# An attention kernel whose per-head stacks and diagonals are filled by transfers through memory instead of by TensorE, for three of its four quartets of batches

## The chip, the cores and the metric

The kernel runs on one core of one Trainium2 chip. The metric is the device time of one execution in microseconds (us); lower is better. Engines: PE (TensorE), DVE (VectorE), ACT (ScalarE), POOL (GpSimd), SP (SyncE, which here only issues transfers). Line numbers (L714) are those of the kernel before.

## What is computed

```python
# x, ctx: (16, 128, 128) f32; 16 heads of 8; mask_BxS2 all ones
x = x + cross_attention(layernorm(x), ctx, ctx, mask, Wq, Wk, Wv, Wo)
#   Q = split_heads(q @ Wq.T), K, V likewise from ctx
#   scores = where(mask == 0, -1e9, Q @ K.T / sqrt(8)); softmax; @ V; @ Wo.T
x = x + moe_ffn(layernorm(x), wg, w1, w3, w2)
#   8 experts, top 2 of softmax(x @ wg.T), silu(x @ w1.T) * (x @ w3.T) @ w2.T
```

## The kernel before

The 16 batches are taken as NQ = 4 quartets of QB = 4 batches; a quartet is T = 512 tokens. Attention runs in rounds u = 0 to 4. In round u PE computes two things side by side, in steps (b, g) with b = 0 to 4 and g = 0 to 3 (a "tick" is 4b + g): for b below 4 the second scores ("S2", L697 and L700) of batch b of quartet u-1, from which ACT takes the exponential (L940); for b of 1 and more the first scores ("S1", L714) of batch b-1 of quartet u, from which DVE takes the maxima (L1431). S1 is used only for the maxima of the softmax; S2 computes the scores again, in the other orientation, with the maxima subtracted by a matmul against m_bd. The maxima of a quartet are turned by PE at the start of the next round (`transpose_maxima`, L545), copied by DVE (mT, L1374) and spread by POOL into m_bd in four steps (L1048). `values` (L673) multiplies the probabilities with V, and three more small steps (L556, L562, L569) finish a batch.

Heads have 8 dimensions, and 4 heads share a matmul. A score must be as exact as fp32, but the matmuls take fp32r, which keeps fewer bits; so each operand is split into a high and a low part. A **stack** `st[:, k, g, :]` (k = 0 queries, 1 keys; g = 0 to 3) holds for each of 4 heads 32 rows: the 8 dimensions three times (high, high and low, or high, low and high) and rows for the mask's bias. A **diagonal** `bd_slot(k, n)` holds for batch n the same rows in block diagonal form, 128 x 2048, so that one matmul of 512 columns gives four heads' scores at once. Its zero blocks are cleared once (`clear_diagonal`, ACT L825), and transfers fill the blocks.

How stacks and diagonals come about before: at the start of each round u below 4, `front(u)` (L624) computes all 8 stacks of quartet u on PE: 4 key stacks of 4 matmuls (one for the bias) and 4 query stacks of 3, each 128x512 (`split_product`, L539), with weights whose columns are repeated threefold (`ws_hi`, `ws_lo`). For each stack ACT copies the high part (`st_hi`, L812 and L913) and DVE combines high and low (L1393). SP then issues, per batch and side, 4 transfers of 64 KB each from stack to diagonal (`block_diagonal`, L424 to L436); 3 diagonals for each side rotate. `st` is double: quartet u is written to `st[:, u % 2]`. The tokens of quartet u+1 are normalised by DVE at b = 3 of round u, turned by PE at (4, 0) (`transpose_tokens`), split at (4, 1) and (4, 2) (x_hi on ACT, x_lo on DVE L1361); the masked context is split on ACT at (4, 3) and on DVE after the round (`context_rest`, L1184).

What sets the order: each engine runs its list in order, semaphores join them. SP's list is that of the round loop from L438; PE's is `front(u)` and the double loop over b and g. The banks of PSUM for the small products alternate by a table (`slot_order`). After round 4 comes the expert part (from about 183 us on), which the change leaves alone save for where some tiles lie.

Of the kernel before, what the change touches and what calls it, by code (L numbers as in the profile page):

```python
# [42 lines left out]
P = 128  # L43
# [44 lines left out]
C_N = C_TILE + NT  # L88
# [3 lines left out]
def constants():  # L92
# [28 lines left out]
    hi, lo = split_constant(NEG)  # L121
    for j in range(NJ):
        c[0, C_BIAS + R * j + 24] = hi
        c[0, C_BIAS + R * j + 25] = lo
# [18 lines left out]
def slot_order():  # L143

    order = [("V", 0), ("xT", 0)]
    for u in range(NQ):
        if u:
            order += [("V", u), ("MT", u - 1)]
        order += [("st", u, k) for k in range(2 * NG)]
        order += [("xT", u + 1)] if u + 1 < NQ else [name for tick in EARLY_FILLS for name in EARLY_FILLS[tick]]  # L150
# [21 lines left out]
STACKS = [(0, 0), (1, 0), (1, 1), (1, 2), (1, 3), (0, 1), (0, 2), (0, 3)]  # L172
# [3 lines left out]
def stacks(u):  # L176

    return sorted(STACKS, reverse=True, key=lambda s: s[0]) if u == 0 else STACKS

def program(nc, x, ctx_in, mask, Wq, Wk, Wv, Wo, wg, w1, w3, w2, consts, xg, ys, out):
    slot, bank_of, turn, uses = slot_order()
    with ExitStack() as stack:
# [16 lines left out]
        nokeep = sb("nokeep", [P, 2, T], F32R)  # L201
# [37 lines left out]
        st = sb("st", [P, 2, 2, NG, T], F32R)  # L239
        bd = sb("bd", [P, 6, NG * NJ * P], F32R)  # L240
# [22 lines left out]

        def bd_slot(k, n):

            return bd[:, 3 * (1 - k) + n % 3, :].rearrange("p (g j q) -> p g j q", g=NG, j=NJ)
# [3 lines left out]
        w3_lo = st[:, 0, 1, :, :].rearrange("p g (m c) -> p (g m) c", c=P)  # L270
        wt_hi = [wt[:, 0], wt[:, 2], wt[:, 4]]
        wt_lo = [wt[:, 1], w3_lo, wt[:, 5]]
# [19 lines left out]
        flat = st[:, :, :, :, :].rearrange("p a b g t -> p (a b g) t")  # L292
        g_hi = [flat[:, 8 + k, 0:I] for k in range(GR)]
        g_lo = [flat[:, 11 + k, 0:I] for k in range(GR)]
        t_hi = [flat[:, 14, k * CT:(k + 1) * CT] for k in range(2)]
        t_lo = [flat[:, 15, k * CT:(k + 1) * CT] for k in range(2)]
# [57 lines left out]
        kbd_ready = [sem(f"kbd_ready{k}") for k in range(3)]  # L354
        qbd_ready = [sem(f"qbd_ready{k}") for k in range(3)]
# [25 lines left out]
        def stacks_in(engine, u, is_k):  # L381

            for k, (kind, _) in enumerate(stacks(u)):
                if kind == is_k:
                    taken(engine, ("st", u, k))

        def diagonal_in(engine, k, n):

            engine.wait_ge((kbd_ready if k else qbd_ready)[n % 3], 16 * NJ * (n // 3 + 1) - (32 if k and n % 3 == 0 else 0))
            if k and n == 0:  # L390
                engine.wait_ge(first_half, 32)
# [17 lines left out]
        def _(sp):  # L409
# [11 lines left out]
            for k, w in enumerate((w1, w3)):  # L421
                sp.dma_start(raw[k], w).then_inc(in_w13, 16)

            def block_diagonal(k, n):  # L424

                u, b = divmod(n, QB)
                stacks_in(sp, u, k)
                if n >= 3:

                    sp.wait_ge(s1_full if k else s2_full, NG * (n - 2))  # L430
                else:
                    sp.wait_ge(bd_cleared, 3 if k else 6)
                for j in range(2 if k and n == 0 else NJ):
                    rows = slice(R * j, R * (j + 1))
                    sp.dma_start(bd_slot(k, n)[rows, :, j, :].bitcast(F32), st[rows, u % 2, k, :, b * S:(b + 1) * S].bitcast(F32)  # L435
                                 ).then_inc((kbd_ready if k else qbd_ready)[n % 3], 16)  # L436

            for u in range(NQ + 1):  # L438
                if u == NQ:
                    sp.wait_ge(work_full, slot["V", NQ - 1] + 1)  # L440
                    sp.wait_ge(ck_ready, NQ)
                    sp.dma_start(raw[2], w2).then_inc(in_w2, 16)

                for k, b in ((1, 0), (1, 1), (1, 2), (0, 3), (1, 3)):
                    if k and u < NQ:
                        block_diagonal(1, QB * u + b)
                    if not k and u >= 1:
                        block_diagonal(0, QB * (u - 1) + b)
                if u < NQ:
                    block_diagonal(0, QB * u)  # L450
                    block_diagonal(0, QB * u + 1)
                    block_diagonal(0, QB * u + 2)
# [64 lines left out]
        def _(pe):  # L517
# [106 lines left out]
            def front(u):  # L624
# [14 lines left out]
                if u >= 1:  # L639
                    transpose_maxima(u - 1)  # L640
                for k, (is_k, g) in enumerate(stacks(u)):
                    if k in (1, 3) and u >= 2:
                        (heads_by_dim if k == 1 else project_out)(QB * (u - 1) - 1)
                    o = claim(("st", u, k))
                    if k < 2 and u:
                        pe.wait_ge(max_done, NG * QB * u)
                    if k == 0 and u == 0:
                        pe.wait_ge(ws_ready, 2)
                    if not is_k and g == 0:
                        taken(pe, ("xT", u))  # L650
                    if is_k and g == 0:
                        pe.wait_ge(cklo_ready, u + 1)
                        pe.wait_ge(mask_ready, u + 1)
                        if u == 0:
# [924 lines left out]
```

## Time and profile before

| | us |
|---|---|
| median of 2 runs | 274.03 (273.87 to 274.19) |
| the profiled execution's own time | 272.4 |
| its span, first to last instruction | 270.6 |
| mean granted clock of PE | 0.908 |

| engine | busy us | share |
|---|---|---|
| PE | 207.4 | 77% |
| DVE | 212.7 | 79% |
| ACT | 132.0 | 49% |
| POOL | 110.0 | 41% |

The shares are means over stages with different limits, so the stages have to be read one by one. The first S1 matmul of rounds 1, 2 and 3 starts at 49.78, 80.40 and 112.02 us of the span; round 4 starts near 141 us and ends near 181 us.

### The profile page before, as it was taken

How to read it: one execution, taken by the hardware profiler on the slowest of the kernel's cores; microseconds unless marked ns; L12 is line 12 of the kernel's file. 1: busy time of each engine (PE TensorE's matmuls, PEld its weight loads, DVE VectorE, ACT ScalarE, POOL GpSimd, SP SyncE). 2: the span in 40 equal slices, each digit the busy share in tenths (PEclk: the TensorE clock that was granted, in tenths of full speed). 3: DMA queues.
4: the chain of work that ended last, by engine and by line, in shares of the span. 5: the costliest groups of instructions: out<-in, count | busy, mean ns of one | idle time of the engine just before them, and what ended most of it. 6: DMA issues, size and time to landing. Idle time of an engine off the chain costs nothing.

```text
span 270.6 us, 5291 instructions
## 1 busy us (share of the span) xinstructions
PE 207.4 (77%) x1445; PEld 154.7 (57%) x1445; DVE 212.7 (79%) x619; ACT 132.0 (49%) x292; POOL 110.0 (41%) x122
## 2 busy tenths in 40 slices
PE   0795779899989989878749884427759999999810
PEld 0572267566756657555525553326658889888600
DVE  4869977498668896789787768786898778888796
ACT  5779037555475636635216773402435555655400
POOL 4401424040602107010749764627336556655630
PEclk9996589999999999999977999555999999999985
DMA  7974420344123320333260210035143322320807
GB/s 229 286 296 115 123 74 13 97 103 114 32 58 98 87 70 0 80 97 99 72 204 13 78 47 24 29 78 138 50 89 85 91 68 79 88 69 19 258 17 225
DMA packets 38108, 26.33 MB, mean 97 GB/s; under 512 B 4748, under 2 KB 35726, under 8 KB 37696
## 3 DMA queue, kind: packets, MB, share of 16 engines
q1 hardware_dynamic: 34848, 19.76, 26.9%
q0 software_dynamic: 2656, 5.40, 6.4%
q10 hardware_dynamic: 576, 0.83, 1.0%
q8 instruction: 13, 0.21, 0.3%
q14 instruction: 15, 0.12, 0.2%
HBM read 12.32 MB, written 6.31 MB: 69 GB/s over the span
## 4 chain that ended last, share of the span: by engine, by line
PE 53%; DVE 32%; issue 6%; DMA 4%; SPq 2%; ACT 2%; POOL 1%; DVEq 0%; ACTq 0%
PE bank L539 8%; DVE m_neg L1431 6%; PE bank L778 4%; PE bank L673 4%; PE bank L697 4%; PE bank L751 4%; PE bank L754 3%; PE bank L700 3%; PE bank L752 3%; PE bank L714 3%; PE bank L779 3%; PE bank L764 3%; DMA bd<-st 2%; DVE st L1393 2%; SPq L435 2%
## 5 line engine op out<-in xcount | busy, mean ns | idle before, releaser
L1431 DVE TENSOR_REDUCE m_neg<-bank 128x4 f32<-128x512 f32 x64 | 43.3, 683 | 14.4 <-PE bank L714 14.2
L1073 POOL DMA_INDIRECT ys<-big x39 | 38.2, 979 | 31.9 <-DVE big L1471 18.0
L940 ACT ACTIVATE big<-bank 128x512 f32<-128x512 f32 x64 | 36.9, 597 | 19.0 <-PE bank L700 18.7
L812 ACT ACTIVATE st<-bank 128x128 fp32r<-128x128 f32 (+1 forms) x78 | 21.9, 329 | 24.8 <-PE bank L764 15.4
L714 PE MATMUL bank<-bd,st 128*128 128x512 f32 x64 | 30.3, 497 | 4.6 <-DMA bd<-st 3.6
L1026 POOL DMA_INDIRECT xg<-rows,rows_i x24 | 24.3, 1011 | 22.8 <-DVE rows_i L1258 15.9
L697 PE MATMUL bank<-m_bd,ones_b 128*128 128x512 f32 x64 | 29.9, 468 | 2.9 <-ACT big L940 2.9
L1393 DVE SCALAR_TENSOR_TENSOR st<-st_hi,cst,bank 128x512 fp32r<-128x512 f32 x32 | 23.3, 748 | 9.6 <-ACT st_hi L812 7.3
L1048 POOL TENSOR_TENSOR m_bd<-mT,cst 128x512 fp32r<-128x512 f32 x16 | 17.3, 1108 | 33.0 <-DVE mT L1374 33.0
L700 PE MATMUL bank<-bd,st 128*128 128x512 f32 x64 | 25.8, 403 | 0.0
L982 ACT ACTIVATE big<-bank 128x256 f32<-128x256 f32 x39 | 15.0, 385 | 19.4 <-PE bank L754 19.4
L778 PE MATMUL bank<-bd,st 128*128 x78 | 22.5, 310 | 1.9 <-DVE big L1471 1.9
L1535 DVE TENSOR_TENSOR big<-big,bank 128x256 f32<-128x256 f32 x39 | 16.4, 421 | 9.4 <-ACT big L982 9.4
L751 PE MATMUL bank<-bd,st 128*128 x39 | 19.7, 505 | 4.8 <-DVE st L1459 4.8
L714 PEld LDWEIGHTS bank<-bd,st 128*128 128x128 f32 x64 | 13.8, 220 | 13.2 <-issue 6.8
L1009 POOL TENSOR_SCALAR ve<-mv 128x4 f32<-128x4 f32 (+2 forms) x9 | 2.4, 269 | 45.5 <-DVE mv L1100 40.9
L779 PE MATMUL bank<-bd,st 128*128 x78 | 20.3, 282 | 0.0
L697 PEld LDWEIGHTS bank<-m_bd,ones_b 128*128 128x128 f32 x64 | 12.8, 200 | 10.4 <-issue 5.7
L1464 DVE TENSOR_TENSOR st<-bank,st 128x256 fp32r<-128x256 f32 x39 | 16.5, 424 | 2.2 <-ACT st L812 1.3
L673 PE MATMUL bank<-big 128*32 128x128 f32 x512 | 17.3, 276 | 0.5 <-DVE x_all L1189 0.5
L778 PEld LDWEIGHTS bank<-bd,st 128*128 128x128 f32 x78 | 14.6, 188 | 4.7 <-issue 3.9
L1471 DVE TENSOR_REDUCE big<-bank 128x128 f32<-128x256 f32 x39 | 16.3, 418 | 0.4 <-PE bank L779 0.4
(175 smaller groups left out, 504.5 us busy)
## 6 DMA issues: line engine op xcount, KB each, us to landing
bd<-st SPq DMA_DIRECT2D x126, 64.0 KB, 2.0
big<-xg SPq DMA_DIRECT2D x39, 64.5 KB, 2.0
raw<-in_L_ffn_w SPq DMA_DIRECT2D x2, 1024.0 KB, 9.4
raw<-ys SPq DMA_DIRECT2D x6, 256.0 KB, 4.6
x_all<-in_x SPq DMA_DIRECT2D x4, 256.0 KB, 4.2
rows<-in_mask_BxS_if POOLq DMA_DIRECT2D x4, 256.0 KB, 5.0
ctx_all<-in_L_ffn_w SPq DMA_DIRECT2D x1, 1024.0 KB, 5.4
ctx_all<-in_ctx SPq DMA_DIRECT2D x3, 256.0 KB, 5.0
```

What stands on the lines that cost most here:

```text
L673: last = nc.tensor.matmul(ob[n % 2][R * j:R * (j + 1), half * P:(half + 1) * P], va[(n // QB) % 2][:, ((n % QB) * 4 + half * 2 + i) * NJ + ...
L697: nc.tensor.matmul(s2[k % 2][:, :], ones_b[:, b, :], m_bd[:, NJ * g:NJ * (g + 1), :].rearrange("p h q -> p (h q)"), start=True, stop=False)
L700: nc.tensor.matmul(s2[k % 2][:, :], st[:, (u - 1) % 2, 1, g, b * S:(b + 1) * S], bd_slot(0, n)[:, g, :, :].rearrange("p j q -> p (j q)"), ...
L714: nc.tensor.matmul(s1[k % s1_ring(u)][:, :], st[:, u % 2, 0, g, (b - 1) * S:b * S], bd_slot(1, n)[:, g, :, :].rearrange("p j q -> p (j q)" ...
L751: nc.tensor.matmul(both, t_lo[n % 2], first_high[:, :, bass.ds(col[n], I)], start=True, stop=False)
L778: nc.tensor.matmul(o, g_hi[n % GR][:, c * P:(c + 1) * P], w, start=(c == 0), stop=False)
L779: last = nc.tensor.matmul(o, g_lo[n % GR][:, c * P:(c + 1) * P], w, start=False, stop=(c == 1))
L940: nc.scalar.activation(prob[n % 2][:, NJ * g:NJ * (g + 1), :].rearrange("p h q -> p (h q)"), s2[k % 2][:, :], ACT.Exp, scale=SCALE).then_i ...
L1026: pool.indirect_dma_start(xg, bass.IndirectOffsetOnAxis(rows_i[:, n, k:k + 1], 0), sent_rows(n // QB)[:, n % QB, k, :], None, bounds_check ...
L1073: pool.indirect_dma_start(ys, bass.IndirectOffsetOnAxis(xt[n % XR][:, D:RW].bitcast(I32), 0), y_sb[n % YR], None, bounds_check=PAIRS - 1, ...
L1393: nc.vector.scalar_tensor_tensor(st[:, u % 2, is_k, g, :], st_hi[:, n % SH, :].bitcast(F32), cst[:, (C_CK if is_k else C_CQ):(C_CK if is_k ...
L1431: nc.vector.tensor_reduce(m_neg[:, H * (b - 1) + NJ * g:H * (b - 1) + NJ * (g + 1)], s1[k % s1_ring(u)][:, :].rearrange("p (j q) -> p j q" ...
```

## The change

Round 0 is as before. For quartets 1 to 3 (the diff's quartets 2 to 4) the 8 stacks are no longer computed:

- PE computes queries and keys once (`queries(u+1)` at tick (2, 2) of round u, `keys(u+1)` at (2, 3); 3 matmuls of 128x512 each), with compact weights `once_w` (two ACT copies after round 0's stacks).
- ACT copies the high parts (`queries_high`, `keys_high`, at (2, 3) and (3, 0)), DVE makes the low parts and the bias rows (`queries_rest`, `keys_rest`, ticks 12 and 13), into `staged`, which lies where the weights w1 and w3 are loaded.
- ACT issues four transfers of 512 KB to a new tensor `qk` in memory: `write_high` twice at (3, 1), `write_low` twice at (3, 3). `qk[u-1, k]` is [128, 4, 512]: each head dimension with its four rows.
- SP issues 4 transfers of 256 KB from `qk` for a whole stack side (`load_stack`) and 4 of 128 KB for the diagonals of a pair of batches (`diagonals`). `st` is single now, so `load_stack(u+1, 0)` waits until all S1 of quartet u are done, and `load_stack(u, 1)` until all S2 of quartet u-1 are. 8 diagonal buffers (2 pairs per side) take the place of 6.
- SP's order in a round: query diagonals of the pair 2u, key stack of quartet u, key diagonals of the first pair of quartet u+1, query stack of quartet u+1, query diagonals of pair 2u+1, key diagonals of the second pair. The loads of w1 and w3 move from the start to the end of this list in round 2.
- The preparation of the next quartet moves ahead: mean and variance to ticks 0 to 2 (for quartet 1 to before round 0's loop), masks to ticks 3 and 4, normalising to 5 and 6, `transpose_tokens` to (1, 3), the context's split to (1, 3) and tick 8, the tokens' to (2, 0) and tick 9.
- `clear_values(1)` moves to DVE's start; POOL clears the two new buffers (`memset` of 128x4096); some tiles of the expert part lie elsewhere.

```diff
+            def queries(u):
+                o = claim(("qc", u))
+                taken(pe, ("xT", u))
+                pe.wait_ge(once_ready, 1)
...
+            def write_high(u, k):
+                act.wait_ge(hi_staged, 2 * u - 1 + k)
+                places = qk[u - 1, k][:, 0:3:2, :] if k else qk[u - 1, k][:, 0:2, :]
+                act.dma_start(places, compact[k][0].unsqueeze(1).to_broadcast([P, 2, T])).then_inc(kc_written if k else qc_written, 16)
+
+            def write_low(u, k):
+                taken(act, ("kc" if k else "qc", u))
+                places = qk[u - 1, k][:, 1:4:2, :] if k else qk[u - 1, k][:, 2:4, :]
+                act.dma_start(places, staged[:, 3 * (1 - k) + 1:3 * (1 - k) + 3, :]).then_inc(kc_written if k else qc_written, 16)
...
+            def diagonals(k, m):
+                u, half = divmod(m, 2)
+                if m >= 2:
+                    sp.wait_ge(s1_full if k else s2_full, 2 * NG * (m - 1))
...
+                if u:
+                    sp.wait_ge(kc_written if k else qc_written, 32 * u)
+                else:
+                    stacks_in(sp, k)
+                tokens = slice(2 * S * half, 2 * S * (half + 1))
+                for j in range(NJ):
+                    rows = slice(R * j, R * (j + 1))
+                    source = rows_of(u, k, j)[:, :, tokens] if u else st[rows, k, :, tokens].bitcast(F32)
+                    sp.dma_start(bd_pair(k, m)[rows, :, j, :].bitcast(F32), source).then_inc((kbd_ready if k else qbd_ready)[m % 2], 16)
...
+            def load_stack(u, k):
+                sp.wait_ge(kc_written if k else qc_written, 32 * u)
+                sp.wait_ge(s2_full if k else s1_full, NG * QB * u)
...
+                for j in range(NJ):
+                    sp.dma_start(st[R * j:R * (j + 1), k, :, :].bitcast(F32), rows_of(u, k, j)).then_inc(kst_ready if k else qst_ready, 16)
...
+            for u in range(NQ):
+                if u:
+                    diagonals(0, 2 * u)
+                    load_stack(u, 1)
+                if u + 1 < NQ:
+                    diagonals(1, 2 * u + 2)
+                    load_stack(u + 1, 0)
+                if u:
+                    diagonals(0, 2 * u + 1)
+                if u + 1 < NQ:
+                    diagonals(1, 2 * u + 3)
+                if u + 2 == NQ:
+                    for k, w in enumerate((w1, w3)):
+                        sp.dma_start(raw[k], w).then_inc(in_w13, 16)
```

PE's wait before the first S1 of a round is now for `stack_loaded(pe, u, 0)` (4 landings of the query stack) and `diagonal_in` (4 landings of the pair of key diagonals).

## Rows read from the trace of the kernel before

**Rows 1.** Part 2 of the page, span in 40 slices.
```profile
PEclk9996589999999999999977999555999999999985
```

**Rows 2.** Stretches: length, busy PE, PEld, DVE, ACT, POOL; PEclk, DMA share, GB/s.
```profile
49.80:67.20 17.40, 17.04 (x185) 11.49 (x185) 14.54 (x38) 9.60 (x21) 3.13 (x4) 1.00 0.43 106
67.20:80.40 13.20, 11.74 (x54) 8.27 (x53) 8.79 (x19) 8.45 (x17) 4.40 (x4) 1.00 0.17 44
80.40:97.50 17.10, 16.62 (x185) 11.54 (x185) 14.21 (x37) 9.29 (x20) 2.57 (x3) 1.00 0.36 94
97.50:112.00 14.50, 12.08 (x55) 8.30 (x54) 11.35 (x32) 8.64 (x18) 5.66 (x6) 1.00 0.13 35
```

**Rows 3.** Chain that ended last, 62 to 83 us: start, length, what.
```profile
70.12 2.08 PE bank L539 x8
...
75.21 0.76 DVE st L1393
...
76.10 0.58 SPq L435
...
78.02 2.05 DMA bd<-st
...
80.40 0.47 PE bank L714
80.87 0.23 PE bank L697
```

**Rows 4.** Timeline, 62 to 98 us, by engine.
```profile
66.76 0.48 PE L714 MATMUL bank<-bd,st 128*128 128x512 f32 x1
...
69.36 4.40 POOL L1048 TENSOR_TENSOR m_bd<-mT,cst 128x512 fp32r<-128x512 f32 x4 [10.39 <-DVE mT L1374]
...
88.76 0.40 PE L697 MATMUL bank<-m_bd,ones_b 128*128 128x512 f32 x1
...
93.04 0.39 PE L700 MATMUL bank<-bd,st 128*128 128x512 f32 x1
...
96.15 0.68 DVE L1361 TENSOR_TENSOR x_lo<-bank,x_hi 128x512 fp32r<-128x512 f32 x1
...
97.39 0.48 PE L714 MATMUL bank<-bd,st 128*128 128x512 f32 x1
```

**Rows 5.** One line's instructions, L435 (issue of the diagonals).
```profile
L435 SPq DMA_DIRECT2D bd<-st x126: 585/601/1547, 19.3 to 149.2; - x126
...
DMA to landing us min/median/max: 2.0/2.0/4.5
```

**Rows 6.** Issues of part 6: KB each, median us from issue to landing.
```profile
out<-ctx_all SPq DMA_DIRECT2D x3, 256.0 KB, 3.1
```

**Rows 7.** Busy time by stretch where DMA share is near 1 (columns as Rows 2).
```profile
15.00:18.00 3.00, 3.00 (x13) 2.43 (x12) 1.82 (x3) 1.49 (x3) 0.00 (x0) 1.00 1.01 411
264.00:268.00 4.00, 0.00 (x0) 0.00 (x0) 3.72 (x14) 0.00 (x0) 0.00 (x0) 0.50 0.99 284
```

**Rows 8.** Busy time by single microseconds round clock changes (columns as Rows 2).
```profile
21.00:22.00 1.00, 0.00 (x0) 0.00 (x0) 0.96 (x2) 1.00 (x2) 0.10 (x1) 1.00 0.68 177
...
23.00:24.00 1.00, 1.00 (x3) 0.81 (x4) 1.00 (x1) 1.00 (x1) 0.00 (x0) 0.50 0.40 100
...
36.00:37.00 1.00, 1.00 (x9) 1.00 (x7) 1.00 (x2) 0.00 (x0) 0.00 (x0) 0.75 0.30 78
```

**Rows 9.** Chain that ended last, 138 to 150 us.
```profile
144.79 0.44 PE bank L700
...
145.75 0.62 ACT bd L812
```

**Rows 10.** Timeline, 0 to 50 us: round 0 and first product of round 1.
```profile
22.33 1.76 DVE L1158 MEMSET big<- 128x2048 f32 x1 [0.38 <-issue]
...
22.86 2.04 PE L714 MATMUL bank<-bd,st 128*128 128x512 f32 x4 [2.48 <-DMA bd<-st]
...
49.78 0.47 PE L714 MATMUL bank<-bd,st 128*128 128x512 f32 x1 [0.39 <-DMA bd<-st]
```

More of the change, by code:

```diff
@@ L121, in constants @@
     hi, lo = split_constant(NEG)
+    c[:, C_KB] = np.where(p % HD == 0, hi, np.where(p % HD == 1, lo, 0.0))
+    c[:, C_QB] = p % HD < 2
     for j in range(NJ):
@@ L379, in taken, with stacks_in, stack_loaded @@
             engine.wait_ge(into_sbuf(name), turn[name] + 1)
-        def stacks_in(engine, u, is_k):
-            for k, (kind, _) in enumerate(stacks(u)):
+        def stacks_in(engine, is_k):
+            for k, (kind, _) in enumerate(STACKS):
                 if kind == is_k:
-                    taken(engine, ("st", u, k))
-        def diagonal_in(engine, k, n):
-            engine.wait_ge((kbd_ready if k else qbd_ready)[n % 3], 16 * NJ * (n // 3 + 1) - (32 if k and n % 3 == 0 else 0))
-            if k and n == 0:
-                engine.wait_ge(first_half, 32)
+                    taken(engine, ("st", k))
+        def stack_loaded(engine, u, is_k):
+            if u:
+                engine.wait_ge(kst_ready if is_k else qst_ready, 16 * NJ * u)
+            else:
+                stacks_in(engine, is_k)
+        def diagonal_in(engine, k, n):
+            m = n // 2
+            if k and m == 0:
+                engine.wait_ge(first_ready[n], 16 * NJ if n else 32)
+                if n == 0:
+                    engine.wait_ge(first_half, 32)
+            else:
+                engine.wait_ge((kbd_ready if k else qbd_ready)[m % 2], 16 * NJ * (m // 2 + (0 if k and m % 2 == 0 else 1)))
         x_d = x.rearrange("(u b) s d -> u s b d", b=QB)
@@ L438, in _, with first_diagonal @@
[L438 to L452, printed above, removed]
+            def first_diagonal(n):
+                stacks_in(sp, 1)
+                sp.wait_ge(bd_cleared, 2)
+                for j in range(NJ if n else 2):
+                    rows = slice(R * j, R * (j + 1))
+                    sp.dma_start(bd_slot(1, n)[rows, :, j, :].bitcast(F32), st[rows, 1, :, n * S:(n + 1) * S].bitcast(F32)
+                                 ).then_inc(first_ready[n], 16)
@@ new lines, in rows_of @@
+            def rows_of(u, k, j):
+                return qk[u - 1, k].rearrange("(g j d) t c -> j (d t) g c", g=NG, j=NJ)[j]
+            def load_stack(u, k):
+                sp.wait_ge(kc_written if k else qc_written, 32 * u)
+                sp.wait_ge(s2_full if k else s1_full, NG * QB * u)
+                if u == 1 and not k:
+                    for m in range(2):
+                        diagonal_in(sp, 0, 2 * m)
+                for j in range(NJ):
+                    sp.dma_start(st[R * j:R * (j + 1), k, :, :].bitcast(F32), rows_of(u, k, j)).then_inc(kst_ready if k else qst_ready, 16)
@@ L638, in front @@
                     context_values(u)
[L639 removed]
                     transpose_maxima(u - 1)
[L641 to L647, printed above, removed]
+                    if u >= 2:
+                        heads_by_dim(QB * (u - 1) - 1)
+                        project_out(QB * (u - 1) - 1)
+                    return
+                for k, (is_k, g) in enumerate(STACKS):
+                    o = claim(("st", k))
+                    if k == 0:
                         pe.wait_ge(ws_ready, 2)
                     if not is_k and g == 0:
[L650 removed]
+                        taken(pe, ("xT", 0))
                     if is_k and g == 0:
[L652 to L655 removed]
+                        pe.wait_ge(cklo_ready, 1)
+                        pe.wait_ge(mask_ready, 1)
+                        pe.wait_ge(setup_ready, 2)
                     parts = (ws_hi[:, is_k, g, :], ws_lo[:, is_k, g, :])
                     if is_k:
[L658 removed]
+                        last = split_product(o[:, :], parts, (ck_hi[:, :], ck_lo[:, :]), (bias_w[:, :], nokeep[:, :]))
                     else:
@@ L722, in _ @@
                             (heads_by_query, heads_by_dim, project_out)[g - late](QB * (u - 1) + b - 2)
-                        if (b, g) == (4, 0) and u + 1 < NQ:
+                        if u + 1 < NQ and (b, g) == (1, 3):
                             transpose_tokens(u + 1)
+                        if u + 1 < NQ and (b, g) == (2, 2):
+                            queries(u + 1)
+                        if u + 1 < NQ and (b, g) == (2, 3):
+                            keys(u + 1)
                         if u + 1 == NQ:
@@ L1163, in _ @@
             clear_values(0)
+            clear_values(1)
             dve.wait_ge(in_x[0], 16)
```

283 lines of the change are left out of this document (175 added, 108 removed).

## The prediction, made before the changed kernel ran

> **What bounds the kernel now.** I read the page's 40 slices first, then the busy time by stretch, then the chain of waits round one turn of a round, then the timeline. The mean shares hide that rounds and the gaps between them have different limits. From the first S1 matmul of a round to its last, PE is the bound: busy 17.04 of 17.40 us and 16.62 of 17.10 us, DVE 14.5 and 14.2, ACT under 10 [rows 2]. In the gap that follows (13.2 us in the second, 14.5 us in the third) the transfer engines are almost empty, at shares of 0.17 and 0.13 [rows 2]. Its chain is: stack matmuls of 0.23 us each (28 of them, 6.4 us), the last stack on DVE 0.76, issues on SP of 0.58 and more, 2.05 us for the landing, then S1 [rows 3]. The first S1 matmuls stand at 49.78 [rows 10] and 80.40 us [rows 3], and the third stretch ends where the next one comes, at 112.0 [rows 2]: turns of 30.6 and 31.6 us. The change empties this gap of its matmuls. PE's clock is at the full 2.4 GHz from slice 7 to slice 21 [rows 1].
>
> I measure a turn from S3, the start of b = 3: in round 2 that is 88.76 us, 8.4 us after the first S1; the last S2 matmul ends at 93.4 (S3 + 4.7), and the last S1 begins at 97.39 (S3 + 8.6) [rows 4].
>
> **What is removed.** Per gap 28 matmuls (6.4 us of PE), 8 ACT copies, 8 DVE combines. What is then late on the compute side is POOL's m_bd, 4.40 us for its four parts, ending at 73.76 where the last S1 began at 66.76 [rows 4]: last S1 + 7.0, and S1 could start at + 7.6 (two S2 matmuls and a handover more). That would be S3 + 16.2, against 88.76 to 112.0 = S3 + 23.2 now. So the change can gain up to 7 us a turn there, if the data have landed by then.
>
> **What is added on the transfers' path.** ACT can issue the high parts only at (3, 1), after the exponential of (3, 0) and two copies: S3 + 1.9. An issue of this kind costs 0.60 us [rows 5]. The low parts wait in ACT's list for (3, 3): ACT takes them at S3 + 5.2 (4.4 by the exponentials' pace, 0.8 for what was put ahead of them) and is done at S3 + 6.4. Behind these issues stand the exponentials, on which PE's S2 depends, but at b = 3 the path runs through the transfers anyway. Bytes: 4 x 512 KB written, beside them the key stack of 1 MB (free to go after the last S2); after the writes have landed, 0.5 MB of key diagonals and 1 MB of query stack. Together 4.5 MB where the gap moved 13.2 us x 44 GB/s = 0.6 MB before [rows 2].
>
> No row has 2 KB pieces in both directions at full load. The nearest: 284 GB/s at share 0.99 with results read and written in 512 B pieces, and 411 GB/s at share 1.01 for weights in 8 KB pieces [rows 7]. I take 350, between them, and keep both ends. A 64 KB transfer lands 2.0 us after its issue [rows 5], a 256 KB one 3.1 [rows 6]; I put 1.2 us before the data and 0.6 after. Then:
> - writes and key stack: data from S3 + 3.1; 3.15 MB at 350 GB/s is 9.0 us, 0.3 us are lost before the low parts arrive: S3 + 12.4, landed S3 + 13.0;
> - SP issues 4 diagonals and 4 stack parts, 8 x 0.6 with 0.04 between; the last issue begins 4.5 us after, and lands 3.1 later: S3 + 20.6.
>
> At 411 GB/s it is S3 + 19.7; at 284 GB/s, S3 + 22.4. Even the fast end is later than POOL's S3 + 16.2: the bound of the gap changes from PE to the transfers.
>
 No row here shows a large one of that kind; by the page's figures the four parts of a stack would take 4.8 us, and the sum would be about 1.5 us longer a turn.
>
> **What is added in the round.** Six matmuls at 0.23 us [rows 3]: 1.4 us of PE, in a stretch that PE bounds; turning the tokens (0.45) moves from b = 4 to b = 1, into the part before S3: together 1.9 us, bounded by 0.5 (hidden in small waits) and 3 (DVE, whose 14.2 us get the low parts and bias rows, some 0.68 each [rows 4], and the context's 0.68: 16.7, so it is near the bound too).
>
> **The clock.** After 2.5 us without a matmul (20.4 to 22.9 us) the granted clock stood at half, 1.2 GHz; it was back within 36 to 37 us, some 2 us after matmuls had become dense again [rows 8, 10]. In the new gap PE has its S2 matmuls and then nothing for some 3 to 4 us before S1. I expect half clock at the start of each round. A matmul of 512 columns then takes 0.44 instead of 0.23 [rows 3, 9]; until the clock returns, 2 to 4 us of PE-bound work go at half speed: 1 to 2 us lost and values with them, 2.0 taken. The Trainium skill says the same of waits for DMA between bursts (TensorE: Matmul & The Clock Gate, HAM oscillation — how this bites in real kernels); the trace agrees for the wait at 21 us.
>
> **Sum of a turn:** 8.4 + 1.9 + 2.0 + 20.6 = 32.9 us, against 30.6 and 31.6: +2.3 and +1.3.
>
> **Into round 1.** Before, DVE took its first maximum at 24.4, held by a memset of 1.76 us [rows 10]. This moves to the start, beside a load that DVE waits for; so S1 maxima run from 23.7. Up to tick 9 come six maxima (0.6 each net), four normalisings (0.33), context and tokens (0.68 each): the tokens are split at 29.2. PE at half clock (0.43 each) has queries, an S1, keys by 32.3, ACT copies by 33.0, and starts the writes at 33.1 (data 34.3). Low parts are issued by 35.4. 2.1 MB at 350 GB/s: 40.3, landed 40.9; then the same 7.6 us: first S1 at 48.5, against 49.78: -1.3. At 284 GB/s it is 49.9. ACT's clearing of the last buffer ends before PE has the queries, so it is not in this sum.
>
> **Into round 3** the half clock costs 1.0 only, since DVE sets the pace there by its routing work. Nothing: the weights' later load (issued near 115 us, used at 145.75 [rows 9]); POOL's memset (it runs while POOL waits for stacks); moved tiles; DVE's statistics of quartet 1 (in DVE's wait for the first stack).
>
> **Total:** -1.3 + 2.3 + 1.3 + 1.0 = +3.3 us on the profiled execution: 272.4 becomes 275.7, its span 270.6 becomes 273.9. The profiled execution lies 1.6 us below the median of the runs, 274.03; on the median's scale the forecast is 277.3.
>
> **Rivals.**
> - *Slower by more: the transfers are slower than the middle.* At 284 GB/s the turns lose 1.8 each and the first entry 1.4: 282.3. If the 32-partition loads go at half rate (205 GB/s: 1.5 MB in 7.7 us + 1.8 where I have 7.6), each of three entries loses 1.9: 283.0; both together 288. For it: 4.5 MB where 0.6 was, written to memory and read back. Against: 411 GB/s were seen. Chance 0.25.
> - *Faster: the transfers land before m_bd is ready, and POOL bounds the gap.* Turns 8.4 + 1.9 + 16.2 = 26.5: -4.1 and -5.1; first entry at last S1 38.6 + 7.6 = 46.2: -3.6; no half clock. 274.0 - 12.8 = 261.2. It decides where writing and reading back take under 14.3 us from S3 + 1.9. Against: low parts are issued by S3 + 6.4, and what must move takes 11.5 us even at 411 GB/s, before any latency. For it: up to 7 us of slack on paper. Chance 0.08.
> - *The clock stays up.* 5.0 us less: 272.3. Against: the wait is longer than the one that halved it at 21 us. Chance 0.12.
> - *As forecast*, 274 to 281: 0.55.
>
> **Range and chances.** 269.5 to 284.5: it holds the forecast, the clock rival and the milder slow ones; outside are the fast rival and both slow causes together. A measurement tells about 2% (5.5 us) from no change. Faster (below 268.5): the fast rival and part of the clock rival with fast transfers, 0.12. Slower (above 279.5): the slow rival and the top of the forecast, 0.35. Within: 0.53.
>
> **What would show it.** In the profile after: no L539 matmuls beyond round 0; first S1 of rounds 1, 2, 3 near 48.5, 81.4 and 114.3 us, each ended by a landing of the query stack; DMA share near 1 in the gaps at 300 to 400 GB/s; PE's last S2 before S1 3 to 5 us earlier, and PEclk 0.5 there. Wrong if: S1 in the gaps waits for m_bd or the key stack rather than the query stack; the writes land before S3 + 11 or after S3 + 15; the clock is 1.0 at the first S1; or the rounds' inner stretches grow by less than 1 us.

## The result, and the profile after

| | before | changed |
|---|---|---|
| median of 2 runs, us | 274.03 (273.87 to 274.19) | 285.63 (284.24 to 287.02) |
| profiled execution, own time / span, us | 272.4 / 270.6 | 287.02 / 285.2 |
| mean granted clock of PE | 0.908 | 0.835 |

The changed kernel takes 1.0399 times the time of before (interval 1.0304 to 1.0494): 4.0% slower, 8 us above the forecast of 277.3 and just above its range. Its profiled execution is 14.6 us longer in span, where the forecast had 3.3. The sign and the bound of the gap (the transfers) were those forecast; the total was near that of the slow rival. A median below is of all runs of a kernel, while a ratio compares only the undisturbed ones (those within about 1.5% of the fastest of each kernel), so the two can differ.

The page's 40 slices, changed kernel:

```profile
PEclk9996666599955998679995798955699999999985
DMA  6806597725997279995088011015332422220717
GB/s 218 257 1 162 128 328 178 163 75 186 270 216 141 76 252 259 212 308 152 9 187 250 20 49 37 9 37 118 90 77 65 112 76 76 87 74 28 215 39 221
```

The clock, full from slice 7 to 20 before [rows 1], now falls in each gap and stays down into the round. The slices of the second and third gap (11 and 12, 16 to 18) have a DMA share of 9 tenths and more where it was 0.17 and 0.13 [rows 2].

What the first-score matmuls wait for, and the chain from the first writes to the first S1 of rounds 2 and 3 (S1 is L783 now, the diagonals' issue L473, the stacks' L487, the high parts' L970, the low parts' L975; columns as in rows 3 and 5):

```profile
L783 PE MATMUL bank<-bd,st x64: 387/466/796, 23.6 to 149.4; 128*128 128x512 f32 x64
  DMA st<-qk: 19.1, 6
```

```profile
34.46 1.29 ACTq L975
35.79 7.82 DMA qk<-raw
43.68 0.34 SPq L473
...
46.90 5.96 DMA st<-qk
52.87 0.04 issue
52.91 0.79 PE bank L783
...
54.98 1.87 PE bank L742 x32
...
58.52 0.62 ACT ck_hi L884
...
59.52 0.60 ACT x_hi L884
...
65.89 0.61 ACT raw L884
66.50 0.24 ACTq L970
...
70.16 5.95 DMA qk<-raw
76.16 0.30 SPq L473
...
79.65 7.16 DMA st<-qk
86.81 0.04 issue
86.85 0.80 PE bank L783
...
104.10 6.41 DMA qk<-raw
...
113.77 7.97 DMA st<-qk
121.74 0.04 issue
121.78 0.50 PE bank L783
```

The first view counts each wait twice, for the weight load and for the matmul: PE itself waits three times, 4.07, 2.25 and 2.33 us before the first S1 of rounds 1, 2 and 3. Both halves of a round trip through memory are on the chain in each turn: the write (landed 5.95 us after its issue in round 1) and the query stack's last part (7.16). The stack computation (L539 before) is gone, as it should be. The first S1 of rounds 1, 2 and 3 stand at 52.91, 86.85 and 121.78 us, where 48.5, 81.4 and 114.3 were forecast and 49.78, 80.40 and 112.02 stood before.

How fast the transfers ran (columns as rows 2; the last two figures are DMA share and GB/s): writes, then the loads into 32 partitions, then two gaps, the first of them also in its last parts (the writes end at 76.10, the loads at 86.81).

```profile
36.00:38.00 2.00, 1.76 (x5) 1.04 (x6) 2.00 (x4) 0.00 (x0) 0.00 (x0) 0.84 1.04 354
38.00:40.00 2.00, 1.65 (x8) 1.35 (x7) 1.93 (x6) 0.32 (x2) 0.00 (x0) 0.50 1.00 309
40.00:42.00 2.00, 0.47 (x1) 0.18 (x1) 1.40 (x9) 0.34 (x2) 0.89 (x1) 0.50 1.00 337
...
46.00:48.00 2.00, 1.99 (x5) 1.00 (x4) 0.00 (x0) 1.28 (x3) 2.00 (x2) 0.60 1.01 232
48.00:50.00 2.00, 0.70 (x2) 0.30 (x2) 0.00 (x0) 1.20 (x2) 0.74 (x2) 1.00 1.04 214
50.00:52.90 2.90, 0.00 (x0) 0.00 (x0) 0.00 (x0) 0.00 (x0) 0.00 (x0) 0.68 1.11 213
...
71.00:86.00 15.00, 10.57 (x65) 6.24 (x64) 8.12 (x25) 5.07 (x12) 6.85 (x7) 0.74 1.05 245
73.00:76.10 3.10, 2.71 (x29) 1.93 (x20) 2.37 (x7) 0.82 (x3) 0.00 (x0) 1.00 1.01 318
76.10:80.00 3.90, 1.60 (x5) 1.03 (x6) 2.23 (x13) 0.67 (x3) 3.19 (x4) 0.79 1.09 215
80.00:86.80 6.80, 4.61 (x10) 2.18 (x9) 1.55 (x2) 2.98 (x5) 3.66 (x4) 0.50 1.08 213
...
104.00:118.00 14.00, 10.41 (x68) 6.48 (x66) 8.14 (x29) 4.33 (x11) 5.26 (x6) 0.80 1.01 246
```

The writes, with what ran beside them, went at 309 to 354 GB/s, about as forecast. With the share as high, the loads moved 213 to 232 GB/s, and a whole gap 245, less than the lower bound of 284. So a share near 1 does not say how fast the bytes flow.

In the round, the stretch from first to last S1 grew from 16.98 to 21.29 us (round 1) and from 16.99 to 21.30 (round 2), while the gap after it shrank only from 13.64 to 12.65 and from 14.63 to 13.63. Its busy PE time rose from 17.04 [rows 2] to 20.17:

```profile
52.91:74.20 21.29, 20.17 (x190) 14.05 (x191) 15.21 (x32) 10.27 (x22) 0.00 (x0) 0.88 0.50 152
```

Before round 4 a second wait shows, on POOL (timeline, changed kernel):

```profile
146.42 1.21 POOL L1143 DMA_INDIRECT xg<-rows,rows_i  x1 [0.30 <-issue]
150.33 0.97 POOL L1143 DMA_INDIRECT xg<-rows,rows_i  x1 [2.69 <-DMA xg<-rows,rows_i]
153.55 0.97 POOL L1143 DMA_INDIRECT xg<-rows,rows_i  x1 [2.25 <-DMA xg<-rows,rows_i]
154.52 4.05 POOL L1167 TENSOR_TENSOR m_bd<-mT,cst 128x512 fp32r<-128x512 f32 x4
```

m_bd stands in POOL's list behind indirect sends, and these wait for the landings of earlier ones, one of which took 7.85 us (the median of the eight before m_bd is 4.5 us, and 3.2 in the kernel before). The second scores of round 4 start at 155.74, 6.30 us after the last S1 at 149.44; before it was 4.93 us (138.10 to 143.03).

### The profile page after: what moved, and what is told of

It is laid out like the page before. It is cut to its first block, busy times and chain, and to the rows that moved or that the text cites. A ratio compares the mean times of both kernels' runs of the same rounds, so it can differ in the third digit from the quotient of the medians.

```text
span 285.2 us, 5017 instructions
## 1 busy us (share of the span) xinstructions
PE 205.8 (72%) x1379; PEld 152.7 (54%) x1379; DVE 205.2 (72%) x604; ACT 121.9 (43%) x277; POOL 113.4 (40%) x123
## 4 chain that ended last, share of the span: by engine, by line
PE 45%; DVE 20%; DMA 19%; issue 6%; SPq 3%; ACT 3%; POOL 2%; ACTq 1%; POOLq 0%; DVEq 0%
DMA st<-qk 7%; DMA qk<-raw 7%; PE bank L597 4%; PE bank L742 4%; PE bank L768 4%; PE bank L850 4%; PE bank L823 4%; DMA xg<-rows,rows_i 4%; PE bank L826 3%; PE bank L771 3%; PE bank L824 3%; PE bank L783 3%; PE bank L851 3%; PE bank L836 3%; DVE ctx_all L1617 2%
## 5 line engine op out<-in xcount | busy, mean ns | idle before, releaser
L1043 ACT ACTIVATE big<-bank 128x512 f32<-128x512 f32 x64 | 37.8, 597 | 45.3 <-PE bank L771 45.1
L1192 POOL DMA_INDIRECT ys<-big x39 | 38.1, 978 | 30.3 <-DVE big L1607 16.5
L1167 POOL TENSOR_TENSOR m_bd<-mT,cst 128x512 fp32r<-128x512 f32 x16 | 16.6, 1070 | 72.0 <-DVE mT L1513 72.0
L768 PE MATMUL bank<-m_bd,ones_b 128*128 128x512 f32 x64 | 36.2, 566 | 7.3 <-DMA bd<-st 3.6
L783 PE MATMUL bank<-bd,st 128*128 128x512 f32 x64 | 29.2, 486 | 12.7 <-DMA st<-qk 8.6
L1143 POOL DMA_INDIRECT xg<-rows,rows_i x24 | 24.8, 1034 | 29.2 <-DVE rows_i L1379 16.9
L771 PE MATMUL bank<-bd,st 128*128 128x512 f32 x64 | 30.8, 482 | 0.0
L768 PEld LDWEIGHTS bank<-m_bd,ones_b 128*128 128x128 f32 x64 | 15.6, 243 | 17.6 <-issue 10.5
L783 PEld LDWEIGHTS bank<-bd,st 128*128 128x128 f32 x64 | 14.4, 229 | 19.5 <-DMA st<-qk 10.5
L742 PE MATMUL bank<-big 128*32 128x128 f32 x512 | 20.2, 307 | 0.5 <-DVE x_all L1310 0.5
L742 PEld LDWEIGHTS bank<-big 128*32 128x32 f32 x512 | 15.0, 123 | 7.2 <-issue 6.2
L826 PEld LDWEIGHTS bank<-bd,st 128*128 128x128 f32 x78 | 15.5, 199 | 3.7
L850 PEld LDWEIGHTS bank<-bd,st 128*128 128x128 f32 x78 | 14.6, 187 | 4.7 <-issue 3.5
L884 ACT ACTIVATE onT<-bank 128x128 f32<-128x128 f32 x16 | 4.4, 277 | 28.5 <-PE bank L620 28.5
```

The source lines that it names most:

```text
L742: last = nc.tensor.matmul(ob[n % 2][R * j:R * (j + 1), half * P:(half + 1) * P], va[(n // QB) % 2][:, ((n % QB) * 4 + half * 2 + i) * NJ + ...
L768: nc.tensor.matmul(s2[k % 2][:, :], ones_b[:, b, :], m_bd[:, NJ * g:NJ * (g + 1), :].rearrange("p h q -> p (h q)"), start=True, stop=False)
L771: nc.tensor.matmul(s2[k % 2][:, :].rearrange("p (j q) -> p j q", j=NJ), st[:, 1, g, b * S:(b + 1) * S], bd_slot(0, n)[:, g, :, :], start=F ...
L783: nc.tensor.matmul(s1[k % s1_ring(u)][:, :].rearrange("p (j q) -> p j q", j=NJ), st[:, 0, g, (b - 1) * S:b * S], bd_slot(1, n)[:, g, :, :] ...
L850: nc.tensor.matmul(o, g_hi[n % GR][:, c * P:(c + 1) * P], w, start=(c == 0), stop=False)
L884: return nc.scalar.activation(o, i, ACT.Copy)
```

## The experiments

All edits are to the changed kernel unless said otherwise. "Entries" are the first S1 of rounds 1, 2, 3; "inner" the time from first to last S1 of a round; the gap is what follows to the next entry. All come from one profiled execution each, ratios from the repeated runs against the kernel before. The rivals: the **ports** (loads into 32 partitions are slow), the **volume** (4.5 MB per gap is too much, wherever it goes), the **clock**.

**a0_changed**: the changed kernel itself, as a base for the others.

> The changed kernel again, unaltered, as the base of this set. Both theories: 284 to 287 us, ratio to before near 1.04, first S1 matmul of rounds 1, 2, 3 near 52.9, 86.9 and 121.8 us of the span.

Measured: 287.54 us, ratio 1.0463 (1.0372 to 1.0553), span 286.0; entries 53.45, 87.54, 121.96; inner 21.25, 20.49, 27.62; gaps 12.84, 13.93.

**a1_wide_stack**: the same bytes of a stack by four transfers that each reach all 128 partitions.

```diff
-                for j in range(NJ):
-                    sp.dma_start(st[R * j:R * (j + 1), k, :, :].bitcast(F32), rows_of(u, k, j))
+                for g in range(NG):
+                    source = qk[u - 1, k].rearrange("(g p) t c -> g (p t) c", g=NG)[g]
+                    sp.dma_start(st[:, k, g, :].bitcast(F32), source)
```

> A stack is loaded by 4 transfers over all 128 partitions (one per g) instead of 4 over 32 partitions each (one per j). Same bytes, same pieces of 2 KB, same number of issues. Theory P (a transfer into 32 partitions can't use all of the transfer engines' rate; the trace of after shows 213 GB/s at share 1.1 while the query stack loads): the query stack lands about 2 us earlier at each of three entries, the key stack too, total 6 to 9 us less than the changed kernel. Theory V (only the bytes count, 4.5 MB at some 245 GB/s): no change, under 1.5 us.

Measured: 278.41 us, ratio 1.0155 (1.0052 to 1.0257): 9.1 us less than a0 by the medians, at the upper end of what was expected. Entries 51.71, 83.64, 115.78; inner 21.11, 21.19, 26.43 (the third 1.2 us shorter than a0's), gaps 10.82 and 10.95. The issues of this kernel (KB each, median us to landing), and its stretches with stack loads in them:

```profile
st<-qk SPq DMA_DIRECT2D x24, 256.0 KB, 4.5
```

```profile
46.00:51.70 5.70, 2.35 (x5) 1.00 (x4) 0.00 (x0) 1.79 (x3) 1.61 (x2) 0.50 1.05 272
69.00:74.20 5.20, 4.72 (x54) 3.23 (x52) 4.55 (x11) 1.42 (x4) 0.00 (x0) 1.00 0.97 319
78.00:83.60 5.60, 3.31 (x9) 1.54 (x7) 2.13 (x8) 2.97 (x5) 4.26 (x5) 0.80 1.06 278
```

The changed kernel had 5.9 us and 213 to 232 GB/s:

```profile
st<-qk SPq DMA_DIRECT2D x24, 256.0 KB, 5.9
```

The second of the three lines has the writes in it, and the changed kernel moved as much in such a stretch (318 GB/s); the loads alone differ, 272 and 278 against 213 to 232. So the edit takes back 9.1 of the 11.7 us that a0's median lies above the kernel before in the same set of runs (275.81). Along the chain, the last part of the query stack took 6.61, 7.95 and 7.46 us to land in a0 and 5.73, 5.88 and 5.33 here: 5.1 us of the 9.4 between the spans. The edit also changes what a transfer reads (256 KB of `qk` that lie together instead of four pieces of 64 KB); no run separates that from the destination. The Trainium skill's rule (SBUF — State Buffer, Door 1: The DMA port swizzle), that 32 partitions reach half of the ports, has the sign right; that the transfer engines work by share at 1.1 meanwhile is this trace's addition.

**a2_warm**: PE also runs constant matmuls that nobody reads, eight (round 1) or ten among the small steps at a round's start and nine before the wait for the query stack.

```diff
+            def keep_busy(count):
+                for _ in range(count):
+                    nc.tensor.matmul(s1[0][:, :], bias_w[:, :], ones_b[:, :, :].rearrange("p b q -> p (b q)"), start=True, stop=True)
...
                                 if b == 1:
+                                    if u:
+                                        keep_busy(9)
                                     stack_loaded(pe, u, 0)
```

> PE gets extra matmuls of constant tiles into a bank that the next S1 overwrites: 3, 2 and 5 after the small steps at the start of rounds 1 to 3 and 9 before the wait for the query stack. They compute nothing that is used. Theory C (half clock at the rounds' starts costs about 2 us each): the clock is 1.0 at the first S1 of rounds 2 and 3, and the stretch from first S1 to last S1 is 1 to 2.5 us shorter each; total 3 to 6 us less. Rival (the wait for the transfers takes back what PE gains, or the clock costs little): under 1.5 us.

Measured: 284.43 us, ratio 1.0347 (1.0257 to 1.0437), 3.1 us less than a0; clock 0.880 against 0.841. Inner 20.63, 20.61, 26.50. The first entry, 55.44, was 2 us later than a0's in this execution, and from there to the last S1 it took 93.1 us where a0 took 96.1. The inner stretches are 0.6 us shorter, 0.1 longer and 1.1 shorter than a0's, less than the 1 to 2.5 us each that were expected, so only a part of the gain lies where the theory put it. The clock is a cause of the loss, worth about a third of what a1 gave back.

**a3_no_key_stack**: leaves out the three loads of later key stacks, so that S2 of quartets 2 to 4 multiplies with round 0's keys; 3 MB less are moved, 1 MB in each of three gaps (before rounds 2, 3 and 4). PE's wait for that stack goes too; in the changed kernel it held the second scores by 1.06 and 0.51 us in the gaps of rounds 1 and 2.

```diff
                     diagonals(0, 2 * u)
-                    load_stack(u, 1)
```

> Leaves out the three loads of the key stack (1 MB each): S2 of quartets 1 to 3 uses round 0's key stack, so the scores are those of other keys. Theory V (the key stack runs beside the writes and holds them up): the writes of quartets 2 and 3 land 2.5 to 4 us earlier and so do the first S1 of rounds 2 and 3; round 1's entry is unchanged; total 5 to 8 us less. Theory L (a chain of fixed latencies, write, receipt, issue, landing): entries of rounds 2 and 3 move by under 1 us.

Measured: 277.19 us, ratio 1.0111 (0.9997 to 1.0226): 10.4 us less than a0. Entries 53.05, 84.07, 112.68: the first, which has no key stack ahead of it, did not move; the two turns went from 34.1 and 34.4 to 31.0 and 28.6. Median landings fell from 4.7 to 4.0 us (writes) and from 5.5 to 3.1 (diagonals). The volume is a cause too, as large as the shape and overlapping with it, for the key stack is itself one of the loads into 32 partitions.

**b1_key_late**: a1, and the key stack is loaded a round ahead into a second buffer (the stacks' weights `ws_hi` and `ws_lo` are done with after round 0), last in SP's list (the lines for the buffer are left out here).

```diff
                 if u:
                     diagonals(0, 2 * u)
-                    load_stack(u, 1)
                 if u + 1 < NQ:
                     diagonals(1, 2 * u + 2)
                     load_stack(u + 1, 0)
...
                 if u + 1 < NQ:
                     diagonals(1, 2 * u + 3)
+                    load_stack(u + 1, 1)
```

> On top of the 128-partition stack loads: the key stack gets a second buffer (where the weights of round 0 lie) and is loaded last in SP's list of a round, after the query stack and all diagonals, a round before it is used. Same bytes in all, but 1 MB less between the writes and the query stack's landing, for quartets 2 and 3. Theory V2 (what is in flight beside the writes sets their landing): first S1 of rounds 2 and 3 come 2 to 3 us earlier each against a1, total 272 to 275 us. Rival L (the writes are held by their own chain, not by company): under 1 us each, 277 to 279.

Measured: 276.40 us, ratio 1.0009 (0.9962 to 1.0057). Entries 51.30, 82.65, 111.40; gaps 9.60, 9.72. The turns are 0.6 and 3.4 us shorter than a1's where 2 to 3 each were expected; the median is 2.0 us under a1's, from another set of runs, and above the 272 to 275 of the theory.

**b2_query_first**: b1, with the query stack issued before the key diagonals, the four diagonal parts in the order 0, 2, 1, 3 (neighbours in the list then lie in different halves of the partitions), and the load of w2 held back until m_bd of the last quartet is written.

```diff
                 if u + 1 < NQ:
-                    diagonals(1, 2 * u + 2)
                     load_stack(u + 1, 0)
+                    diagonals(1, 2 * u + 2)
...
             sp.wait_ge(ck_ready, NQ)
+            sp.wait_ge(mbd_ready, NG * NQ)
             sp.dma_start(raw[2], w2)
```

> On top of b1: SP loads the query stack before the key diagonals (the queries are written first, so it need not wait for the keys' writes), diagonals go in the order j = 0, 2, 1, 3 (neighbours in the queue then use different partition halves), and the load of w2 waits until POOL has spread the maxima of round 4. Expected by theory P and V2: another 0.5 to 1.5 us at each of three entries, and POOL's m_bd of round 4 no longer behind its transfers: 1 to 1.4 us less there. Total 268 to 272. Rival (entries are then set by the keys' writes alone, whatever comes in which order): 271 to 274.

Measured: 273.37 us, ratio 0.9937 (0.989 to 0.9984). Entries 51.86, 82.79, 111.90; gaps 9.66, 9.41; round 4's S2 starts 4.7 us after the last S1, as before the change. Its chain of waits at the end of the gap of round 1:

```profile
77.37 0.41 PE bank L776
77.78 0.43 PE bank L779
...
81.36 0.24 PE bank L779
81.60 1.19 issue
82.79 0.47 PE bank L791
```

The ten S2 matmuls of the gap (L776, L779) run from 77.37 to 81.60 without a wait, most of them at half clock (0.43 us), and only 1.19 us are left before S1, for which the profile names no releaser. From S3 (65.94 in this kernel's timeline) to S1 it is 16.9 us, where the fast rival had 16.2; but that rival had POOL's m_bd as the bound, and here PE doesn't wait for it. The entries are not earlier than b1's, against the 0.5 to 1.5 us each that were expected, and this profiled span (274.0) is longer than b1's (271.5): where the median's 3.0 us against b1 come from isn't shown. The total, 273.37, lies in the rival's range.

**b3_alternate**: the changed kernel with only the order 0, 2, 1, 3, for stacks and diagonals.

```diff
-                for j in range(NJ):
+                for j in (0, 2, 1, 3):
```

> The changed kernel with one edit: the four transfers of a stack and of a pair of diagonals are issued in the order j = 0, 2, 1, 3 instead of 0, 1, 2, 3. Bytes, pieces, partitions per transfer and issues are the same. Theory P in its sharper form (partitions 0 to 63 and 64 to 127 have separate ways in, so neighbours of different halves overlap and neighbours of one half don't): 3 to 7 us less than the changed kernel. Rival (any transfer into 32 partitions is slow, whichever its neighbour, by what its own shape costs): under 1.5 us.

Measured: 285.87 us, ratio 1.0367 (1.029 to 1.0444), 1.7 us under a0's 287.54 from the other set of runs; the intervals of the two ratios overlap. That is near the rival's end, and under the 3 us at which the theory began: the order of the parts does little, if anything.

**b4_lighter_act**: b2, with the high part of the masked context copied by POOL and the low parts sent one step earlier.

```diff
+                if u:
...
+                    nc.gpsimd.tensor_copy(ck_hi[:, :], ck[:, :]).then_inc(ckhi_ready, 1)
...
-                            if (b, g) == (3, 3):
+                            if (b, g) == (3, 2):
                                 write_low(u + 1, 0)
```

> On top of b2: ck_hi of quartets 1 to 3 is rounded by POOL instead of ACT, and the low parts are sent one step earlier, at (3, 2). Theory A (ACT's added copies stand in front of exponentials on which PE waits): the stretch from first S1 to b = 3 is 0.6 to 1 us shorter in rounds 1 and 2, and the writes land up to 1 us earlier: 1.5 to 3.5 us less than b2. Rival (PE and DVE bound the stretch anyway): under 1 us.

Measured: 276.08 us, ratio 0.994 (0.9873 to 1.0007). Turns 30.3 and 28.8 against b2's 30.9 and 29.1; but the same kernel as b2 had 29.5 and 28.8 in another execution (d1), so this shows no gain, and the ratios show none.

**c1_early_w2** and **c2_early_w2_busy**: b4 with the load of w2 as in the changed kernel, and that with a2's constant matmuls (ten, and five before the wait).

> The kernel of b4_lighter_act with one edit taken back: the load of w2 again goes out as soon as the last masked context is written, not after m_bd of the last quartet. Theory (the load of w2 paid for nothing by waiting: round 4's entry got 0.5 us, but the expert part later waited for w2): last first S1, 110.6, and last S1, 137.3, unchanged; first S2 of round 4 later by 0.5 to 1.5 us after the last S1 (wait of 5.4 to 6.4 instead of 4.9); from there to the end 128 to 129 us instead of 130.85; total 1 to 2 us less than b4's 276.1, a ratio to the kernel before of 0.986 to 0.992. Rival (the longer rest of b2 and b4 comes from the clock in round 4 or is scatter between executions): rest stays at 130 to 131, and the total is b4's or up to 1 us more.

> As c1_early_w2, and in each gap PE also runs constant matmuls whose results nobody reads: 3, 2 and 5 among the small steps at a round's start and 5 before the wait for the query stack. Theory (the clock's share of the loss is the same as in a2_warm, about 1 us a round, and is independent of the transfers): mean granted clock up by 0.03 to 0.04, each stretch from first to last S1 shorter by 0.7 to 1.1 us, total 1.5 to 3 us below c1_early_w2. Rival (the shorter gap of these kernels has its idle time before S1 too short to halve the clock, or the added matmuls stand in front of the second S2 product that the gap now contains): total within 1 us of c1_early_w2 or above it.

Measured: c1 275.07 us, ratio 1.0031 (0.9994 to 1.0067). Its profile did what the theory said (wait for round 4's S2 5.24 us, 128.8 us from there to the end against b4's 130.9), its total did not. c2 278.71 us, ratio 1.0187 (1.0129 to 1.0246), slower than c1, though the clock of the profiled executions rose from 0.862 to 0.882. In the gap of round 1 of c1 and of c2:

```profile
76.00:83.50 7.50, 5.27 (x15) 2.60 (x15) 3.77 (x14) 3.42 (x7) 6.83 (x7) 0.77 1.05 274
```

```profile
76.00:83.00 7.00, 6.47 (x31) 4.41 (x33) 3.67 (x13) 2.94 (x6) 6.28 (x7) 1.00 1.10 258
```

The clock is 1.00 there instead of 0.77, but PE is now busy 6.47 us of 7.00: there was no long wait left to fill. What made c2's total worse wasn't traced further; its rounds 1 to 3 end 0.6 us after c1's (139.47, 138.88).

**d1_query_first_again** and **d2_query_first_w2_early**: b2 once more, and b2 without the wait ahead of w2.

> The kernel of b2_query_first, unchanged, once more, beside new runs of the kernel before. If its ratio of 0.994 is the kernel's own, it comes out between 0.989 and 0.999 again. If that was a matter of one set of runs, the ratio is 0.999 to 1.006 here.

> b2_query_first with w2 loaded as in the changed kernel, in the same set of runs as d1. Theory by the times of b4 (0.994, w2 late) and c1 (1.003, w2 early): the early load costs 0.5 to 1 per cent, 1.5 to 2.5 us more than d1, though the profiled executions of b2, b4 and c1 show the rest after round 4's entry shorter with the early load (128.1 and 128.8 against 130.2 and 130.9). Rival by those profiles: the load's place makes no difference, both within 1 us, since what round 4's entry gains the rest gives back.

Measured in one set of runs: d1 275.37 us, ratio 0.9936 (0.9886 to 0.9985); d2 275.87 us, ratio 0.9925 (0.9863 to 0.9986). The place of the w2 load makes no difference in the total. The ratio of b2 came again, as expected (0.9937 and 0.9936, and 0.9925 for the variant). Still, a gain of 0.6% is less than the 2% that was set for the chances, and it rests on which runs are compared: by the medians of all runs b2 was 2.6 us under the kernel before, but d1 only 0.6 and d2 0.1 under it (275.99).

## Why the prediction was off, step by step

**What held.** The gap's bound is the transfers: each first S1 of rounds 1 to 3 waits for the query stack, and the time goes with the bytes (a3) and their shape (a1). The matmuls that went left no gain: PE waits at that place now. The clock was at half at the first S1 of rounds 1 and 2 (0.79 and 0.80 us a matmul). At that of round 3 it was still 1.00 (121 to 122 us) and fell to 0.50 by 123, one of the signs of being wrong that the prediction had named. A reading of [rows 1] was off by one: slice 21 has 7 tenths, the full clock ends with slice 20.

**Right by luck.** From S3 to S1 20.6 us were forecast; measured from 67.01, the start of b = 3, to 86.85 it was 19.8, and in the next turn (100.96 to 121.78) 20.8. Two errors cancel in it. The writes were to land at S3 + 13.0 and landed at 76.10 and 110.51, which is S3 + 9.1 and S3 + 9.6. This too is a named sign of being wrong (before S3 + 11). The low parts were issued by S3 + 3.7, not 6.4, and landed 5.4 and 5.9 us after that where 6.6 were allowed. What this gave, the loads behind it took.

**The failed steps**, in the changed kernel's profiled execution, which missed the forecast span by 11.3 us:

- *"the last issue begins 4.5 after, and lands 3.1 later"*, the 7.6 us from the landed writes to S1, used for all three entries. They were 9.3, 10.7 and 11.3 us: 1.7, 3.1 and 3.7 more. The issues were cheap (the last load was out 3.2 to 3.6 us after the writes had landed); the landing was mis-sized, 5.96, 7.16 and 7.97 us for 3.1. The 3.1 is the median of three transfers that go the other way, the writes to `out` at the kernel's end [rows 6], while the loads of that size at its start, in the same page of the kernel before, had 4.2 and 5.0:

```profile
x_all<-in_x SPq DMA_DIRECT2D x4, 256.0 KB, 4.2
ctx_all<-in_ctx SPq DMA_DIRECT2D x3, 256.0 KB, 5.0
```

  No rate entered this term, so its ends at 284 and 411 GB/s did not widen with it. By the rows above, some 2.3 MB went from 76.1 to 86.8 us, at 213 to 215 GB/s, where 1.5 MB had been counted: the rest of the key stack (issued until 73.5) and query diagonals (issued from 80.2) went beside them. I had priced the ports at 1.9 us an entry, in a rival. In a1 the two turns were 2.2 and 2.3 us shorter than a0's. Its first entry came 1.7 us sooner, but its writes had landed 0.9 us sooner already, before any load of the new shape: 0.9 is left for the shape. Behind the last entry came 3.2 us more (spans 286.0 and 276.6), of which 1.2 lie in round 3.
- *"2.1 MB at 350 GB/s: 40.3, landed 40.9"*, the entry into round 1, which was 4.4 us late in all. The writes landed at 43.6: 2.7 us, and the loads' 1.7 make up the rest. The rate was near the one assumed (309 to 354 GB/s from 36 to 42 us), but a neighbour was left out: 1 MB of round 0's query diagonals, issued from 30.9 until 37.9 us, was in the engines beside the writes. No run moves them away.
- *"together 1.9 us"* and *"2.0 taken"*, from first S1 to S3: 14.1 us in rounds 1 and 2 where 12.3 was forecast, +1.8, and more than both upper bounds together (3 and 2, which give 13.4). The whole stretch from first to last S1 was nearly right, +4.3 us for 3.9, since its part behind S3 shrank from 8.6 to 7.2. In the chain ACT's copies of context and tokens (0.62 and 0.60 us) and of queries and keys (0.61) stand between exponentials that PE waits for, and at half clock values takes 1.87 us instead of 1.01. b4, which took one copy off ACT, did not show the copies' price. The turns were +1.0 and +2.0: in the first, S3 to S1 gave 0.8 back. In the second it was 1.0 longer than in the first; the loads of w1 and w3, which I had put at nothing, are issued at 118.04 us there, while the query stack is still landing. Whether they did it wasn't tried.
- *"Into round 3 the half clock costs 1.0 only"*: 27.66 us against 26.08 before: 1.6, so +0.6.
- Not in the forecast at all: round 4. Its S2 starts 1.4 us later after the last S1, because POOL's m_bd stands behind its indirect sends and these behind SP's loads of that stretch. The key stack is the one that counts: a3, which only leaves out the key stacks, has 4.4 us where a0 has 6.0, and its m_bd waits for DVE and no longer for a send. The load of w2 alone makes 0.2 us (5.1 in d2, 4.9 in d1). And S2 takes 19.9 us from first to last (155.74 to 175.68) where it took 17.8 (143.03 to 160.80). In the profile the clock is at 0.57 in its first 5 us after the idle stretch, at 0.52, where before it stood at 0.73 after 0.58:

```profile
149.80:155.70 5.90, 2.53 (x7) 1.15 (x6) 4.23 (x17) 0.78 (x3) 3.12 (x4) 0.52 0.96 297
155.70:161.00 5.30, 5.26 (x12) 2.81 (x12) 4.95 (x15) 3.26 (x7) 5.02 (x6) 0.57 0.01 4
```

  I read the 1.9 us that the rest lost, from the first S2 of round 4 to the end, from this; no run tests it alone.

The sum of the misses: 4.4 + 1.0 + 2.0 + 0.6 + 1.4 + 1.9 = 11.3 us. Some 3 us of it is scatter: this execution lay 1.4 us over the median of its runs, the one before 1.6 under. On the medians 8.3 us are left.

**The rivals.** The slow one came true, by its second cause, the loads into 32 partitions (priced 283.0, and 288 with the general rate at 284 GB/s as well; 285.63 measured). That 285.63 lies near these is in part chance: the loads' miss was 1.7, 3.1 and 3.7 us where 1.9 each was priced, the writes' came in between, and round 4 was in neither. Its first cause in that form did not hold: where the writes ran at a share near 1, the engines moved 298 to 354 GB/s. The reason given against it, 411 GB/s, was of a transfer of another shape. The clock did not stay up; keeping it up by a2's extra matmuls gave 3.1 us, where I had put 5.0 on it. The fast rival's 16.2 us from S3 to S1 were nearly reached in b2 (16.9), though with PE at half clock and not POOL as what fills the gap, and its 261.2 was not: b2's gaps of 9.66 and 9.41 us are 4.0 and 5.2 shorter than before, but its inner stretches of 21.27, 19.70 and 27.22 are 4.3, 2.7 and 1.1 longer, and the first entry is 2.1 us later. In sum the last S1 is 1.0 us later than before (139.12 and 138.10), and in d1, the same kernel, 0.4 earlier (137.72). What the gaps win, the rounds pay.

## What to carry to other kernels

Where a change puts a transfer on the critical path behind others, its time to land is not that of a lone transfer of its size: take it from a row with the same direction and company, or from the bytes ahead of it at the lowest rate seen, and let that term widen with the range. A DMA share near 1 tells nothing of bytes, so read GB/s beside it, and let a bulk load reach all 128 partitions. Count what else is in the transfer engines at that time: loads that nobody waits for yet (here the key stack, and probably round 0's diagonals) delay those that somebody does. When a forecast stretch comes out right, check its parts: here the writes came 3 to 4 us early and the loads took them up. And work moved out of a gap into a stretch that PE bounds is paid for there: with six matmuls more, the copies between exponentials and the half clock at the start, each of these stretches became 4.3 us longer; only the clock's part was tried alone (a2).

## What the runs showed that I had not expected

- The same 256 KB took 5.9 us to land when they went to 32 partitions and 4.5 when they went to 128, with the DMA share at 1.01 to 1.11 and 213 to 232 GB/s in the first case, and at 1.05 to 1.06 and 272 to 278 GB/s in the second.
- Four transfers into different quarters of the partitions, put in another order in one queue, changed the time by 1.7 us only, at the edge of what the runs tell.
- Indirect sends of POOL took up to 7.85 us to land beside SP's bulk loads, and at most 4.8 in d1, where the key stack and w2 are loaded at another time (5.4 in the kernel before). This is as the Trainium skill has it (DMA: Bandwidth & Descriptors, Issuing engines are not separate DMA queues): they share the engines, whoever issues them.
- A higher mean clock is not a shorter time: in the profiled executions c2's was 0.02 above c1's, and its ratio was 1.0187 against 1.0031.
